# An attention and feed-forward block on one core: smaller selects, moved copies and stores, and unused products in five steps

## The reference

```
mod = (silu(c) @ wmod)  ->  sa, ca, ga, sb, cb, gb          (per image, 256 each)
h   = layernorm(x) * (1 + ca) + sa
q, k, v = h @ w_in.T, 16 heads of 16;  scores = q k / 4, causal;  attn = softmax(scores)
x   = x + ga * ((attn v) @ w_out.T + b_out)
h   = layernorm(x) * (1 + cb) + sb
hp  = h shifted by one token (zero first)
r   = sigmoid((mu_r h + (1 - mu_r) hp) @ W_r.T);  k = relu((mu_k h + (1 - mu_k) hp) @ W_k.T)^2
out = x + gb * (r * (k @ W_v.T))
```

## Time and profile before

| | |
|---|---|
| median of 3 runs | 1612.03 us (1609.94 to 1618.19) |
| the profiled execution's own time | 1611.15 us |
| its span | 1609.4 us, mean granted PE clock 0.919 |
| busy: PE, DVE, ACT, POOL | 1426.9, 1055.5, 985.6, 663.2 us |
| first attention step of image 0 | at 76.4 us |
| the steady part, images 1 to 6 | 248.1 to 1364.8 us |
| last product of the last attention quarter | ends at 1540 us |

### The profile page before, as it was taken

The page is one execution under the profiler, slowest core; times in us unless marked ns, Lnnn a source line. Parts: engine busy times, 40 slices in busy tenths (PEclk is TensorE's granted clock), DMA queues, the critical chain, the costliest instruction groups (busy, mean ns, idle before and its releaser), DMA issues.

```text
span 1609.4 us, 30222 instructions
## 1 busy us (share of the span) xinstructions
PE 1426.9 (89%) x10856; PEld 809.6 (50%) x10856; DVE 1055.5 (66%) x2099; ACT 985.6 (61%) x1972; POOL 663.2 (41%) x874
## 2 busy tenths in 40 slices
PE   5898999889998989889998999989998899999855
PEld 4543445445554556445554556545564455544444
DVE  7766667766677767766677667766667666766233
ACT  2167556656667666676567666676566666656533
POOL 4013122553436344553445444444445534343554
PEclk9598889989999999999899999989899999988778
DMA  4321123122321223222231223211232222211000
GB/s 135 83 48 43 38 63 95 42 61 58 82 83 45 58 56 111 63 51 52 69 96 45 58 68 101 69 44 48 64 104 60 56 56 73 66 51 49 35 28 27
DMA packets 79509, 101.92 MB, mean 63 GB/s; under 512 B 22512, under 2 KB 43256, under 8 KB 79360
## 3 DMA queue, kind: packets, MB, share of 16 engines
q1 hardware_dynamic: 76544, 91.86, 21.9%
q0 software_dynamic: 2240, 7.34, 1.3%
q10 hardware_dynamic: 576, 0.79, 0.3%
HBM read 30.69 MB, written 8.94 MB: 25 GB/s over the span
## 4 chain that ended last, share of the span: by engine, by line
PE 57%; POOL 11%; ACT 10%; DVE 9%; issue 7%; SPq 4%; DMA 3%; ACTq 0%; POOLq 0%; DVEq 0%
PE val_ps L1273 14%; PE col_ps L1204 13%; PE row_ps L1241 9%; PE dense_ps L1283 7%; ACT weights L805 5%; PE dense_ps L1284 5%; PE dense_ps L1285 5%; SPq L495 4%; DVE max_a L1021 3%; POOL weights L657 3%; PE row_ps L1252 2%; DMA xq<-in_x 2%; PE dense_ps L1302 1%; POOL mix_out L734 1%; ACT h_hi L845 1%
## 5 line engine op out<-in xcount | busy, mean ns | idle before, releaser
L805 ACT ACTIVATE weights<-col_ps 128x512 f32<-128x512 f32 (+2 forms) x1280 | 642.3, 555 | 394.1 <-PE col_ps L1204 386.3
L1021 DVE TENSOR_REDUCE max_a<-row_ps 128x1 f32<-128x512 f32 (+3 forms) x896 | 537.6, 645 | 225.9 <-PE row_ps L1252 122.6
L1204 PE MATMUL col_ps<-q_stack,k_stack 64*128 64x512 f32 (+3 forms) x1536 | 401.5, 430 | 30.2 <-ACT weights L805 28.8
L657 POOL TENSOR_SCALAR_AFFINE_SELECT weights<-weights 128x512 f32<-128x512 f32 x256 | 169.4, 662 | 550.9 <-ACT weights L805 550.5
L1273 PE MATMUL val_ps<-weights,v_ones 128*32 128x512 f32 (+3 forms) x3072 | 355.8, 537 | 39.7 <-POOL weights L657 39.2
L1241 PE MATMUL row_ps<-k_stack,q_stack 62*128 62x512 f32 (+3 forms) x1536 | 355.0, 441 | 23.5 <-DVE max_a L1021 15.7
L1021 DVE TENSOR_REDUCE max_b<-row_ps 128x1 f32<-128x384 f32 (+3 forms) x384 | 214.9, 596 | 199.9 <-PE row_ps L1252 199.6
L1204 PEld LDWEIGHTS col_ps<-q_stack,k_stack 64*128 64x128 f32 x1536 | 199.8, 197 | 199.1 <-ACT weights L805 179.7
L1241 PEld LDWEIGHTS row_ps<-k_stack,q_stack 62*128 62x128 f32 x1536 | 170.3, 198 | 229.5 <-DVE max_a L1021 119.3
L1252 PE MATMUL row_ps<-mask_fill,mask_ident 64*128 64x128 bf16 (+1 forms) x2048 | 134.1, 215 | 0.0
L1273 PEld LDWEIGHTS val_ps<-weights,v_ones 128*32 128x32 f32 x3072 | 62.1, 111 | 131.6 <-POOL weights L657 66.3
(11 more groups left out here) (200 smaller groups left out, 2116.0 us busy)
## 6 DMA issues: line engine op xcount, KB each, us to landing
q_stack<-q_part SPq DMA_DIRECT2D x384, 64.0 KB, 2.2
k_stack<-k_part SPq DMA_DIRECT2D x372, 64.0 KB, 2.2
xa<-in_x SPq DMA_DIRECT2D x8, 1024.0 KB, 5.9
att<-val_out SPq DMA_DIRECT2D x64, 128.0 KB
recips<-recip_rows SPq DMA_DIRECT2D x32, 256.0 KB
xq<-in_x SPq DMA_DIRECT2D x28, 256.0 KB, 3.3
out<-xq POOLq DMA_DIRECT2D x28, 256.0 KB, 2.6
q_stack<-max_rows SPq DMA_DIRECT2D x256, 4.0 KB
```

The source lines that it names most:

```text
L657: nc.gpsimd.affine_select(out=w, in_=w, compare_op=ALU.is_ge, fill=0.0, base=0, pattern=[[0, G], [1, P]], channel_multiplier=-1).then_inc( ...
L805: nc.scalar.activation(weights[:, t % 2, heads[0]:heads[-1] + 1:2, 0:q1 - q0], col_ps[bank][:, 0:n * (q1 - q0)].rearrange("p (h q) -> p h ...
L1021: nc.vector.reduce_max(dest, bank[:, 0:len(heads) * (k1 - k0)].rearrange("p (h k) -> p h k", h=len(heads)), AX_X).then_inc(max_done, 1)
L1204: last = nc.tensor.matmul(col_ps[bank][:, i * (q1 - q0):(i + 1) * (q1 - q0)], stack_at(k_stack[s % 2], rows, heads[i], P * j, P * (j + 1)) ...
```

## The change

- **PE**: a new `keep_clock` issues three 512-column products of fixed weights into the dense bank, whose result nobody reads, after a wait that the bank is empty. It is called at the end of steps (s, t) = (1, 4), (2, 3), (3, 3), (3, 4), (3, 5) where maxima for a next quarter are formed: 40 times in all.
- **POOL**: a select is made in two halves of two heads each, the first waiting only for half of the step's exponentials. The parts of tick 15 move into `finish`, behind the select of their step. The store of a quarter goes from POOL to SP.
- **ACT and DVE**: `h_full` is written by DVE, after ACT has written `h_hi` of the same bank; DVE now frees the bank. ACT's `normalise` for "norm" moves from the end of tick 5 to the middle of tick 6, and for "transposed" from the end of the step before to the middle of its own step. DVE's second blend moves from tick 8 to tick 9.
- **DVE**: maxima are written straight into spare columns of `max_parts`, `max_a` and `max_b` go, and `split_max` works with reductions in place of a `tensor_scalar` and a `scalar_tensor_tensor`.

```diff
+IDLE_STEPS = ((1, 4), (2, 3), (3, 3), (3, 4), (3, 5))
...
+            def keep_clock(last_dense):
+                if last_dense:
+                    pe.wait_ge(free[last_dense[2]], last_dense[3])
+                for _ in range(3):
+                    nc.tensor.matmul(dense_flat, w_hi[:, 0:P], w_hi[:, 0:HALF], start=True, stop=True)
...
+                    if has_rows(kind, s) and (s, t) in IDLE_STEPS:
+                        keep_clock(before[0])
...
             def select(b, s, t):
-                wait_apart(pool, "pool", exp_done, exp_index(b, s, COL_FIRST[t + 1]))
-                w = weights[:, t % 2, :, 0:P]
-                nc.gpsimd.affine_select(out=w, in_=w, ..., pattern=[[0, G], [1, P]], channel_multiplier=-1)
+                c0, c1 = COL_FIRST[t], COL_FIRST[t + 1]
+                for part in range(2):
+                    wait_apart(pool, "pool", exp_done, exp_index(b, s, c0 + (c1 - c0) // 2 * (part + 1)))
+                    heads = slice(2 * part, 2 * part + 2) if c1 - c0 == 4 else slice(part, G, 2)
+                    w = weights[:, t % 2, heads, 0:P]
+                    nc.gpsimd.affine_select(out=w, in_=w, ..., pattern=[[0, 2], [1, P]], channel_multiplier=-1)
...
                     if attends(kind) and t in DIAGONAL:
                         select(b, s, t)
+                    for item in at:
+                        finish(*item)
...
-                        nc.gpsimd.dma_start(out_tiles[b - 1:b, :, 2 * s:2 * s + 2, :], xr
-                                            ).then_inc(out_stored[s % 2], 16)
+            def store_quarter(b, s):
+                hold(out_done, quarters(b, s) + 1)
+                sp.dma_start(out_tiles[b - 1:b, :, 2 * s:2 * s + 2, :], residual(b, s)).then_inc(out_stored[s % 2], 16)
...
-                    wait(act, h_lo_done, count - 1)
-                    for c in range(KC):
-                        nc.scalar.activation(h_full[:, c, :], dense_ps[:, c, :], ACT.Identity, ...)
...
+                if unit and unit[0] == "transposed":
+                    dve.wait_ge(h_hi_done, count)
+                    wait(dve, h_lo_done, count - 1)
+                    for c in range(KC):
+                        last = nc.vector.tensor_scalar(h_full[:, c, :], dense_ps[:, c, :], mod[:, 2 + c:3 + c],
+                                                       mod[:, c:c + 1], ALU.mult, ALU.add)
+                    last.then_inc(free["transposed"], 1)
...
+                    for c in units[:2]:
+                        exps(b, s, t, c)
+                    for item in at:
+                        between(*item)            # u == 6: the normalise that stood at the end of u == 5
+                    normalise_next(b, kind, s, t)
+                    for c in units[2:]:
                         exps(b, s, t, c)
...
-                if u == 8:
+                if u in (8, 9):
+                    m = u - 8
...
-                nc.vector.tensor_scalar(hi, src, -1.0, None, ALU.mult)
-                nc.vector.scalar_tensor_tensor(lo, src, -1.0, hi, ALU.mult, ALU.subtract)
+                    nc.vector.tensor_reduce(parts[:, 0:16], whole..., AX_X, ALU.max, negate=True)
+                    nc.vector.tensor_reduce(parts[:, 16:32], pairs, AX_X, ALU.add, negate=True)
```

More of the change, by code:

```diff
@@ L579, in body @@
                         spread_recips(b - 1, 1)
+                    if s == 0 and kind in ("mid", "last", "drain"):
+                        store_quarter(b - 1, G - 1)
+                    if s > 0 and backs(kind) and kind != "drain":
+                        store_quarter(b, s - 1)
                     if attends(kind):
@@ L882, in empty_dense, with between @@
                     nc.scalar.activation(relu_of(b), dense_of(b, s), ACT.Relu).then_inc(free["key"], 1)
+            def between(b, s, u):
+                q = quarters(b, s)
+                if u == 6:
+                    wait(act, ready["norm"], q)
+                    normalise(residual(b, s), rstd_c, shift_c, xn_c, shift_c_done, xn_c_done, q + 1)
             def split(b, s, u):
@@ L889, in split @@
                     nc.scalar.activation(o_hi[:], att_n[:, :, QT * s:QT * (s + 1)], ACT.Copy).then_inc(o_hi_done, 1)
-                if u == 5:
-                    wait(act, ready["norm"], q)
-                    normalise(residual(b, s), rstd_c, shift_c, xn_c, shift_c_done, xn_c_done, q + 1)
                 if u == 9:
@@ L909, in body @@
                         empty_dense(*item)
-                    for c in range(COL_FIRST[t], COL_FIRST[t + 1]) if attends(kind) else ():
+                    units = range(COL_FIRST[t], COL_FIRST[t + 1]) if attends(kind) else ()
+                    for c in units[:2]:
[4 more added lines that the diff above has]
+                    for c in units[2:]:
                         exps(b, s, t, c)
@@ L1019, in maximum @@
                 first = 2 * (heads[0] % 2) + heads[0] // 2
-                dest = (max_b[:, i - 4] if second else max_a[:, i])[:, first:first + len(heads)]
+                half = i // 4
+                col = MAX_COLS[half + second] + 4 * first + i % 4
+                dest = max_parts[half][:, col:col + 4 * len(heads) - 3:4].bitcast(F32)
                 nc.vector.reduce_max(dest, bank[:, 0:len(heads) * (k1 - k0)].rearrange(
@@ L1064, in front, with rest_of_front @@
                                     b * 4 + (4 + k + 1))
-            def rest_of_qk(b, kind, s, t):
+            def rest_of_front(b, kind, s, t):
                 unit = front_unit(b, kind, s, t - 1)
+                if unit and unit[0] == "transposed":
+                    _, k, count = unit
+                    mod = mod_t[:, 8 * (b + 1):8 * (b + 1) + 4]
+                    dve.wait_ge(h_hi_done, count)
[3 more added lines that the diff above has]
+                                                       mod[:, c:c + 1], ALU.mult, ALU.add)
+                    last.then_inc(free["transposed"], 1)
                 if unit and unit[0] == "qk":
```

56 lines of the change are left out of this document (27 added, 29 removed).

## The result

The change takes 1555.4 us, median of 4 runs (1551.16 to 1566.52), beside 1610.99 for the kernel before: a ratio of 0.966 [0.960, 0.972]. The forecast was 1567. The profiled execution took 1554.07 us, with a span of 1552.1.

The account below looks back on a forecast made before the run. It took quarter 1 as bound by ACT, with half-clock stretches after PE's waits and a narrow step 3 costing time too. Terms summed to -45.0 us from 1611.15, giving 1566.1, set at 1567; range 1540 to 1602.

Parts of the forecast that it names:

- signs set down before: Marks in the new profile, such as quarter times, clock, split and select lengths, listed as showing the forecast right or wrong.
- h_full to DVE: Quarter 1 of the six steady images: with ACT relieved it comes near 46.2 us, 26.3 us saved in all.
- the rival of ACT's wait being replaced by DVE's: After transposed units DVE waits for h_hi, maxima come 1.9 us later and PE stops: 1646 us, slower; chance 0.08.
- Clock: Quarters 2 and 3 of the steady images: shorter waits and added products keep full clock, 15 us saved, between 0 and 20.1.
- Added products: Batches in steps 3 to 5: mostly hidden in PE's waits, 0.2 us for each of three, 3.6 us cost in all.
- Select halves: First step of three quarters an image: 0.24 us less wait after the last exponential, 4.3 us saved in all.
- Narrow step 3: Quarters 0, 2 and 3: earlier select and undisturbed split by reductions save 0.5 us each, 8 us counted in all.
- Normalise: ACT's work for "norm" between two pairs of exponentials: 0.3 us more in three quarters an image, 5 us cost in all.
- Store by SP, second blend: Store ahead of SP's copy of the values, and blend one tick later: nothing gained or lost in the steady part.
- Images 0, 7 and the drain: Around the steady images: some 3 us gained from clock and ACT, as much perhaps lost in the drain; together 0.

Follow-up runs that it names:

- run 4: The changed kernel with h_full written by ACT again, ahead of h_hi, and the bank freed by ACT: 1582.3 us, ratio 0.981 to the kernel before.
- run 2: The kernel before with only the 120 unused products added: 1597.2 us, ratio 0.990 to the kernel before.
- run 1: The changed kernel without its 120 unused products: 1552.9 us, ratio 0.963 to the kernel before.
- run 9: The changed kernel without unused products, with the old split and with multiplication and sum ahead of the select again: 1583.61 us, ratio 0.980 to the kernel before.
- run 7: The changed kernel with max_a, max_b and the split by tensor_scalar and scalar_tensor_tensor again: 1553.64 us, ratio 0.962 to the kernel before.
- run 8: The changed kernel with multiplication and residual sum ahead of the step's select again, store still by SP: 1558.18 us, ratio 0.966 to the kernel before.
- run 10: The changed kernel with both blends of DVE in tick 8 again: 1559.54 us, ratio 0.966 to the kernel before.
- 6: The changed kernel with ACT's normalise for "norm" at the end of tick 5 again: 1554.85 us, ratio 0.963 to the kernel before.

## Why the prediction was right, and where its terms were not

The sign, the two largest terms and the quarters were right: 45 us foreseen, 57 in the profiled execution. That the total came so near is in part luck: two terms of 4.3 and 8 us brought nothing that can be seen beside the products, and the ends, put at nothing, brought 18.6. Of the signs set down before, quarter 1 near 46 us with ACT near 33, the split under 0.4, selects near 410 ns and the clock at 1.00 in quarters 2 and 3 came; that steps 4 and 5 would not be moved by a batch did not. By its own steps:

- *h_full to DVE*, -26.3: 22.5 us in quarter 1 (46.8 us, 46.2 foreseen); undone alone, 26.9 in all. Right in size, and the rival of ACT's wait being replaced by DVE's is seen in one step only, up to 1.56 us before PE's first "recept" product. But the term counted ACT's work alone, and the clock term left quarter 1 out, where half clock fell from 61 to 14 us. The gain also needs the halved selects: undone, these alone take 19.5 of the 22.5 back. I had left out that image 0 has these units too; it is 3.5 us longer in run 4, which is less than image 0 differs (156 to 163 us) between the change and runs that hardly touch it.
- *Clock*, -15: quarters 2 and 3 are at 1.00 in all twelve, which took away some 20 us (7.6 and 12.6 against six quarters of 44.2 and 43.2). That is an estimate, as the lengths at full clock differ too; the quarters themselves are 6.8 and 7.9 us shorter. Right mechanism, at its upper end. Which edit did it was not settled by the change at all: products alone do it (run 2), and the other edits without products in eleven quarters of twelve (run 1).
- *Added products*, +3.6: mis-sized. I had taken 0 in step 3 and 0.2 in steps 4 and 5; against the kernel without them a batch costs 0.3 and 0.4 us. ACT's 1.09 us cover only about half of it: the row product behind a batch in step 4 starts 0.88 us after the batch's start, and the step is 0.40 longer, the rest being time that PE would have waited. In quarters 3 they cost 8.4 us less the 3.5 of the one that would lose the clock, 4.9 net. Over the steady images it is 9.1 in the profiled executions, of which 2.5 lie in quarters 0, which hold no batch, so some 6.6 at most can be put down to the products directly.
- *Select halves*, -4.3: the 0.36 at a quarter's start is gone, step 11 to 0 is 0.23 us shorter, and step 8 to 9, which I had not counted, gains as much, but in quarters 2 and 3 step 0 to 1 gives back 0.22 and the sum is unchanged. Undoing them costs 29 us, 19.5 of them in quarter 1, by a collision in one step that the kernel before, with whole selects, did not have. So that is what the halves are worth beside the other edits, not what they gained on the kernel before. Not foreseen.
- *Narrow step 3*, -8: the waits of 0.87 and 0.18 went, but not as said. With the products in place neither the split nor the order shows in the time, and the 0.87 is filled by the batch: without products a wait of 0.74 for DVE's maxima is left, so the faster split took only 0.13 off the last wait, and the extra waits in front of it. Without the products, both edits together are worth 31 us by the medians, 27 by the ratios: some 7 in the steps themselves (0.6 in twelve of them), and much of the rest stands beside 41 us more of half clock, which can be up to 20. The mechanism, a split slowed by POOL that holds PE, is borne out by run 9, with the split at 0.65 to 1.42 us. By the rule of the Trainium skill (SBUF — State Buffer, Who interferes with whom) reductions are not disturbed by POOL; the trace agrees, with 169 to 171 and 186 to 191 ns over 64 each, for up to 1297 in the earlier trace rows. With the new order the time did not hang on it (run 7). The quarters were wrong: I had counted 0, 2 and 3, but in quarter 0 the values of step 3 never waited for the select nor PE for the last maxima, while in quarter 1 of the kernel before they waited 1.13 us for the select (1.31 in image 1), and no longer do.
- *Normalise*, +5: 0.29 in three quarters, where 0.3 was foreseen; undoing it gains that there and loses as much in quarter 1, so that the total does not change. The other moved normalise, for "transposed", was undone by no run.
- *Store by SP, second blend*, 0: by the rows, the store was worth something in quarter 1. There the select of step 3 stood right behind it on POOL, and the values waited for that select; this is POOL in quarter 1 of image 4 of the kernel before:

```profile
864.22 0.82 POOL L739 DMA_DIRECT2D out<-xq  x1 [0.30 <-POOL xq L737]
865.06 0.65 POOL L657 TENSOR_SCALAR_AFFINE_SELECT weights<-weights 128x512 f32<-128x512 f32 x1
```

Here 0.30 and 0.82 us on POOL stand for the wait of 1.13. With multiplication and sum ahead of the select again but the store on SP (run 8), that wait is nothing and step 2 to 3 of quarter 1 takes 3.31 us, as in the change, for 3.96 before: 4.0 us over six images that I had put at nothing. SP's wait for the sum of POOL is new (156.7 us in 28 waits) and that for the values fell to 103.3. PE waits once for a copy that SP issues, 1.05 us in quarter 0 of image 3, which no wait of the kernel before shows, and POOL waits 17.8 us for the residual loads, for 10.3 before. Right for the blend by run 10, whose ratio is that of the change; the store was not undone by itself.
- *Images 0, 7 and the drain*, 0: this is the term that failed. The images gave 25 us, the drain took 4.9. Image 0 ran at clock 0.88 before and 0.97 after. In images 0 and 7 together, products alone give 3 us, the other edits without products 8.7, both 25; half clock stands there for 83 us before, 68 with the products alone, 85 with the other edits alone and 34 with both. So only together do they hold the clock there. These are single executions, but the runs that undo one small part of the change (6, 7, 8, 10) have 323 to 327 us for the two images, near the 322 of the change and not the 338 without products. I had no row of image 0 among those that I argued from.

Of the drain, this much is seen: the low part of the input of "value" (k_lo) of the last quarter but one starts 45.9 us after the last attention product, 41.4 before. Ahead of it stands a pair of blends that takes 1.93 us beside POOL, and 0.88 before. Both chains of waits, after and before:

```profile
1521.80 1.93 DVE mixed L1137 x2
1523.72 0.61 DVE k_lo L1162
```

```profile
1579.19 0.88 DVE mixed L1105 x2
...
1581.46 0.61 DVE k_lo L1130
```

Yet with the blend moved back alone the drain is 74.0 us, and with the normalise moved back alone 74.2, for 74.3 with both late and 69.4 before. It is 74.0 without the products and 69.3 with them alone, so it is not the products, and 73.2 to 74.6 with the split, the selects, the order or h_full undone. Both moves at once, or the store, were not tried; the cause of these 4.9 us stays open.

In sum, the steady images gave 38.7 us where 45 were foreseen, and what lies around them 18.6 (15.6 + 9.3 - 1.4 - 4.9) where nothing was. The first error is 6.3 us, about what the products cost above their term; other terms missed by as much each way and cancel in it. The second is larger, and makes the 12 us by which the profiled execution beat the forecast.

## What to carry to other kernels

Where a clock falls behind short waits, find the waits first: here some half a microsecond less of wait in a narrow step did for quarters 2 and 3 of the steady images what three unused products did, and in quarter 3 one product held the clock as three did at under a tenth of the price. Test such filling in the smallest dose, and where two remedies meet in one step, undo both before calling either useless, and look at the rows of all stretches of a kind before one of them is taken as the case. Compare quarters of one kind with each other, and read the first and last stage as well as the steady one: 25 of these 57 us were there.

## What was not expected of the hardware

- The granted clock fell to 0.50 in or just behind a narrow step in nine of twelve quarters 2 and 3 of run 9, each with two or more waits of PE in the step, such as 0.41 and 0.87 or 0.71 and 0.53 us; the three quarters with a single wait of 0.81 to 0.87 stayed at 1.00, and so did eleven of twelve in run 1, with a single wait of 0.75 at most, which the one that fell had too. No pause of PE in those steps was longer than 0.91 us.
- DVE's blend of two SBUF operands took 453 ns at the least, 478 in the middle and up to 1533 beside POOL's 512-element operations, and POOL's own went from 1.26 to 1.45 us; a pair that met only the end of such an operation and half a select took 1.05 us in the changed kernel, where a pair beside POOL's small operations took 0.88.
- A 128x256 select costs 423 ns in the mean and a 128x512 one 662: two halves are 0.18 us more work for POOL, and the first ends 0.24 earlier.
